# A fused two-layer feed-forward kernel: one product, half of the next narrow product and the gate chain taken at other places of the main stage

## The chip, the cores and the metric

The kernel runs on 1 core of a Trainium2 chip. The metric is the device time of one execution in microseconds: 909.95 us for the kernel before, the median of 3 runs that lie between 909.25 and 910.49 us. The profile comes from one more execution. PE is the matmul engine TensorE (PEld its weight loads), DVE is VectorE, ACT is ScalarE, POOL is GpSimd, SP is the engine that issues most DMAs.

## The reference, cut to what matters

Two blocks act on x of 4096 tokens by 1024 features, in float32. Each is a "cond" layer and a routed adapter layer behind it, with a residual:

```python
x = x + L0_ffn(L0_cond(x))     # cond 0: codebook-quantised weight + low-rank part; ffn 0: base W, bias, top-2 of 8 experts
x = x + L1_ffn(L1_cond(x))     # cond 1: weight, bias, an adapter per sequence of 64 tokens; ffn 1: base W, top-2 of 8 experts

# each routed layer
base   = x @ W.T (+ b)
logits = x @ W_router.T
rw, sel = top_k(logits, 2); rw = softmax(rw)
out    = base + sum over the two experts of rw * (x @ A[e].T) @ B[e] * 2
```

The first cond weight is quantised with `searchsorted` against thresholds made of the 64-entry codebook, in groups of 128 scaled by `exp(scale_log)`.

## The kernel before

Everything that does not depend on the gates is linear, so the kernel first multiplies the weights together: a 1024 x 1024 matrix G (`g_hi`, `g_lo`) and a narrow matrix `gx` with the router and adapter columns. This setup takes the first part of the span. In it, the codebook is brought from one row to all partitions by three groups of tiny matmuls (`codebook_step`, lines 546 to 555) that stand between the matmuls of an ordinary row product; `CB_AT` says behind which chunk. The product `delta(0)` behind that row waits for the copies that VectorE makes of them (`comp_ok`).

Float32 is kept by splitting each operand into a high and a low part (`fp32r`); a product a*b is three matmuls, hi*hi, hi*lo and lo*hi. ScalarE makes the high parts (line 978), VectorE the low ones (line 1310).

**The main stage** takes tiles of T2 = 256 tokens, numbered tau = 0 to 15. Tiles 0 and 1 are plain products. From tau = 2 on (`REG`), `winograd_products` computes a 2 x 2 block product with seven block products in place of eight. Each has 12 matmuls of 512 columns (line 858):

- i = 0 to 11, bank 3: the first of three products with a precomputed block T, which is read back from DRAM. There is room for one T, in two halves (`t_hi`, `t_lo`), so the halves are reloaded three times a tile. PE tells SP by `t_free`, six counts a tile, when a half can be overwritten; SP's program issues the loads (`load_t`) in order between the loads of x and the stores of the output.
- i = 12 to 23, bank 0; i = 24 to 35, bank 3.
- i = 36 to 47, bank 2: the second T product, with `m0_terms` (line 841) ahead and behind it.
- i = 48 to 59, bank 0 again: what this document calls the fifth product. It waits for ScalarE's copy of bank 0 (`p1_ok`).
- i = 60 to 71, bank 1.
- i = 72 to 83, bank 3: the third T product. Behind it VectorE makes a sum of bank 3 (line 1888, `u3_ok`), which waits for `t_free`.

**The gate chain** (`chain`, table `CHAIN`) is threaded into these products by the number i: a transposition of the gated values `m0` (line 775), six narrow matmuls that add them to the narrow banks (788 to 792), a transposition of the per-sequence low-rank values (799), and their product (807). Between these stand ScalarE's and VectorE's steps; the VectorE function `front` (lines 1725 to 1755) does the first gate's top-2 and softmax, `back` (to 1778) the second one's.

**The narrow product** `x_product(tau + 1)` (lines 519 to 521) has 48 matmuls of 304 columns and fills both narrow banks for the next tile. `front(tau + 1)` begins when it is done (`xx_mm`). It stands behind `low_terms` and the transposition of the second gate's values (`mid_turn`, line 775) and ahead of `mid_terms` (932 to 934), which end the tile.

The order on each engine is the order of the code, tile after tile. VectorE's main loop from line 1867 on reads: `m0_low`, `low_rank`, a sum of two partial products, the low part of half the next x, `u4_sum`, `back`, the low part of the other half, the sum behind the third T product (1888), `s_sums` (1821 to 1824, four sums of the next x), `mid_low`, `s_low` (1310), `front` of the next tile, and the output sums (1835) of which the first lies within `front`. ScalarE's loop has `x_high(tau + 1, 1)`, which waits for the fifth product (`p2_mm`), and then `rex`, the exponential in the middle of `back`.

Of the kernel before, what the change touches and what calls it, by code (L numbers as in the profile page):

```python
# [15 lines left out]
KC = D // P  # L16
# [18 lines left out]
CHAIN = [(30, 44, 62, 76), (10, 24, 42, 56), (12, 28, 44, 56)]  # L35
# [13 lines left out]
CB_AT = {(1, 0): 0, (1, 2): 1, (1, 6): 2}  # L49
# [13 lines left out]
def build(nc, xq, wall, m1t, aallt, x0t, b0t, lb1, lorabt, loraa, wq, cbook, ids, packed, out,  # L63
          e_dram, p1_dram, b_dram, t_dram):
    with ExitStack() as ctx:
# [217 lines left out]
        t_free, p1_mm, p2_mm, p6_mm = sem("t_free"), sem("p1_mm"), sem("p2_mm"), sem("p6_mm")  # L283
# [231 lines left out]
        def _(pe):  # L515
# [244 lines left out]
            def x_product(tau):  # L760

                u = tau if tau < REG else 0
                pe.wait_ge(x_hi_s, 2 * tau + 2)
                pe.wait_ge(x_lo_s, 2 * tau + 2)
                pe.wait_ge(gsel_ok, tau + 1)
                for b in range(2):
                    cs, ts = slice(SX * b, SX * b + WX), slice(b * P, b * P + P)
                    for c in range(KC):
                        mm = split_product(xb[:, b, cs], x_hi[u][:, c, ts], x_lo[u][:, c, ts],
                                           gx[:, c, cs], gx[:, 9 + c, cs], c == 0, c == KC - 1)  # L770
                mm.then_inc(xx_mm, 1)
# [71 lines left out]
            def winograd_products(tau):  # L843
# [43 lines left out]

                pe.wait_ge(ev[2], tau)
                m0_terms(2, True)
                t_loaded(0, 1)  # L890
                product(36, 2, quarter(0, 1, 1), (t_hi, t_lo), False, lambda: t_loaded(1, 1)).then_inc(t_free, 1)
# [3 lines left out]
                pe.wait_ge(p1_ok, n + 1)  # L895
                product(48, 0, quarter(0, 0, 1), g_quarter(1, 0), False).then_inc(p2_mm, 1)

                product(60, 1, quarter(1, 0, 1), g_quarter(1, 1), False)
# [50 lines left out]
            for tau in range(REG, NT2):  # L949
                winograd_products(tau)  # L950
                if tau + 1 < NT2:
                    low_terms(tau, (0, 2, 1))
                    mid_turn(tau)
                    low_terms(tau, (3,))
                    x_product(tau + 1)
                    mid_ready(tau)
                    mid_terms()
            last = NT2 - 1
            mid_turn(last)
# [15 lines left out]
        def _(act):  # L975
# [203 lines left out]
            def x_high(tau, k):  # L1179
# [3 lines left out]
                elif tau == REG:  # L1183
                    act.wait_ge(g_all, 1)
                else:
                    act.wait_ge(p2_mm if k else p1_mm, tau - REG)
# [76 lines left out]
            for tau in range(REG, NT2):  # L1263
# [15 lines left out]
                low_turned(tau)  # L1279
                if tau + 1 < NT2:  # L1280
                    x_high(tau + 1, 1)
                rex(tau, 1)
# [677 lines left out]
```

## Time and profile before

| | |
|---|---|
| median of 3 runs | 909.95 us |
| the profiled execution's own time | 910.41 us |
| span, first to last instruction | 908.7 us |
| PE busy | 902.7 us, 99% |
| PEld busy | 787.7 us, 87% |
| DVE busy | 616.3 us, 68% |
| ACT busy | 312.9 us, 34% |
| POOL busy | 145.7 us, 16% |
| granted TensorE clock | 1.0 of full speed in all slices |
| main stage from tau = 2 to 15 | from 433 us to 908 us |

A matmul's busy time overlaps that of the next one: the 512-column matmuls show a mean of about 395 ns and start some 230 ns apart. So the busy share says only that PE hardly ever waits; where time goes or comes from is read from the start times. A tile of the main stage takes about 34 us.

### The profile page before, as it was taken

What the parts mean: (1) busy time and instruction counts of PE and PEld (TensorE: products, weight loads), DVE (VectorE), ACT (ScalarE), POOL (GpSimd) and SP (SyncE); (2) the same over time, 40 slices, a digit from 0 to 9 for tenths busy, and PEclk for the clock granted to TensorE, in tenths of its full rate; (3) what the DMA queues carried; (4) which work ended last, traced back from release to release, by engine and by line L of the source; (5) the groups of instructions that cost most, each with busy time, mean ns of one, the idle gap of its engine ahead of it and who ended that gap; (6) DMA issues with size and microseconds to landing.
All of it is one profiled execution on the core that took longest, in us unless ns stands there. A gap on an engine that the chain in (4) does not pass through costs nothing.

```text
span 908.7 us, 13371 instructions
## 1 busy us (share of the span) xinstructions
PE 902.7 (99%) x4673; PEld 787.7 (87%) x4673; DVE 616.3 (68%) x1312; ACT 312.9 (34%) x503; POOL 145.7 (16%) x298
## 2 busy tenths in 40 slices
PE   9999999999999999999999999999999999999998
PEld 8999998888998888888888888888888888888886
DVE  6889899766587878976455565566566566566563
ACT  6578778411324334231321221222222222222220
POOL 0100010111011001414213213213113113113110
PEclk9999999999999999999999999999999999999999
DMA  9523330765412033657787787888888887877865
GB/s 360 188 82 114 120 125 23 257 193 186 142 50 93 8 131 102 212 208 238 268 290 260 270 285 255 279 277 258 285 276 262 283 272 261 286 268 265 287 221 188
DMA packets 60256, 191.45 MB, mean 211 GB/s; under 512 B 7681, under 2 KB 10394, under 8 KB 58270
## 3 DMA queue, kind: packets, MB, share of 16 engines
q1 hardware_dynamic: 49468, 158.99, 50.7%
q0 software_dynamic: 10432, 31.35, 11.3%
q8 instruction: 37, 0.61, 0.3%
q10 hardware_dynamic: 290, 0.26, 0.1%
q14 instruction: 29, 0.24, 0.1%
HBM read 158.86 MB, written 32.23 MB: 210 GB/s over the span
## 4 chain that ended last, share of the span: by engine, by line
PE 94%; DMA 4%; DVE 1%; SPq 1%; issue 0%; ACT 0%
PE bank L858 28%; PE bank L519 15%; PE bank L521 15%; PE bank L520 15%; PE bank L841 5%; PE bank L832 5%; DMA t_lo<-t_scratch 3%; PE bank L666 2%; PE bank L906 2%; PE bank L933 2%; PE bank L932 2%; PE bank L934 2%; DMA w_raw<-wall 1%; PE bank L775 1%; SPq L311 0%; PE bank L537 0%
## 5 line engine op out<-in xcount | busy, mean ns | idle before, releaser
L858 PE MATMUL bank<-g_hi,xs 128*128 128x512 f32 x448 | 145.2, 395 | 0.0
L858 PE MATMUL bank<-t_hi,xs 128*128 128x512 f32 x336 | 113.4, 396 | 0.6 <-DMA t_lo<-t_scratch 0.3
L490 POOL DMA_DIRECT2D p1sel<-p_scratch x128 | 65.6, 512 | 279.1 <-issue 279.0
L858 PEld LDWEIGHTS bank<-g_hi,xs 128*128 128x128 f32 x448 | 83.2, 188 | 16.4
L858 PE MATMUL bank<-g_lo,xs 128*128 128x512 f32 x224 | 88.2, 394 | 0.0
L978 ACT ACTIVATE xs<-x_raw 128x1024 fp32r<-128x1024 f32 x60 | 61.9, 1056 | 76.1 <-PE bank L858 55.8
L1310 DVE TENSOR_TENSOR xs<-x_raw,xs 128x1024 fp32r<-128x1024 f32 x60 | 75.1, 1273 | 12.0 <-ACT xs L978 11.5
L519 PE MATMUL bank<-gx,xs 128*128 128x304 f32 x256 | 77.4, 302 | 0.0
L521 PE MATMUL bank<-gx,xs 128*128 128x304 f32 x256 | 77.4, 302 | 0.0
L520 PE MATMUL bank<-gx,xs 128*128 128x304 f32 x256 | 77.3, 302 | 0.0
L858 PEld LDWEIGHTS bank<-t_hi,xs 128*128 128x128 f32 x336 | 62.0, 188 | 15.6 <-DMA t_lo<-t_scratch 3.2
L1725 DVE COPY rt<-bank 128x16 f32<-128x16 f32 x32 | 5.6, 174 | 99.0 <-PE bank L807 61.6
L501 POOL COPY bls<-bl 128x16 f32 x64 | 32.4, 506 | 249.0 <-ACT l L978 147.1
L519 PE MATMUL bank<-m_hi,w_hi 128*128 128x388 f32 (+1 forms) x192 | 65.9, 343 | 0.0
L858 PE MATMUL bank<-t_lo,xs 128*128 128x512 f32 x168 | 65.7, 391 | 0.0
L520 PE MATMUL bank<-m_lo,w_hi 128*128 128x388 f32 (+1 forms) x192 | 65.0, 339 | 0.0
L521 PE MATMUL bank<-m_hi,w_lo 128*128 128x388 f32 (+1 forms) x192 | 65.0, 338 | 0.0
L1471 DVE SCALAR_TENSOR_TENSOR rbuf<-qbuf,thr,rbuf 128x1024 f32<-128x1024 f32 x48 | 59.5, 1281 | 4.9 <-ACT rbuf L1029 4.3
L1029 ACT ACTIVATE rbuf<-rbuf,step 128x1024 f32<-128x1024 f32 x48 | 53.8, 1149 | 10.3 <-DVE rbuf L1466 6.8
L519 PE MATMUL bank<-weff_hi,w_hi 128*128 128x512 f32 x128 | 50.3, 393 | 0.0
L521 PE MATMUL bank<-weff_hi,w_lo 128*128 128x512 f32 x128 | 49.9, 390 | 0.0
L520 PE MATMUL bank<-weff_lo,w_hi 128*128 128x512 f32 x128 | 49.8, 389 | 0.0
(325 smaller groups left out, 2061.4 us busy)
## 6 DMA issues: line engine op xcount, KB each, us to landing
t_hi<-t_scratch SPq DMA_DIRECT2D x82, 512.0 KB, 4.5
t_lo<-t_scratch SPq DMA_DIRECT2D x82, 512.0 KB, 5.8
x_raw<-xq SPq DMA_DIRECT2D x16, 1024.0 KB, 6.7
out<-ost SPq DMA_DIRECT2D x63, 256.0 KB, 5.1
p1sel<-p_scratch POOLq DMA_DIRECT2D x64, 192.0 KB, 4.6
w_raw<-wall SPq DMA_DIRECT2D x16, 512.0 KB, 4.9
w<-e_scratch SPq DMA_DIRECT2D x6, 1024.0 KB, 5.1
ea<-e_scratch POOLq DMA_DIRECT2D x8, 644.0 KB, 4.5
```

The costliest lines, as they stand in the source:

```text
L490: pool.dma_start(f(p1sel[b][STK * s:STK * s + STK, cs]), p1_dram[bass.ds(i * STK, STK), cs]).then_inc(sems[b], 16)
L501: nc.gpsimd.tensor_copy(bls[:, b, s, :], bl[:, i, :].squeeze(1))
L519: nc.tensor.matmul(out_ap, lhs_hi, rhs_hi, start=first, stop=False, skip_group_check=True)
L520: nc.tensor.matmul(out_ap, lhs_hi, rhs_lo, start=False, stop=False, skip_group_check=True)
L521: return nc.tensor.matmul(out_ap, lhs_lo, rhs_hi, start=False, stop=last, skip_group_check=True)
L832: mm = nc.tensor.matmul(bk[j][:], l[tau][:, c, b * P:b * P + P], m[:, c, hs], start=c + k == 0, stop=c + k == KC + 1, skip_group_check=True)
L841: nc.tensor.matmul(bk[j][:], vt(l, b), m[:, hs], start=first and k == 0, stop=k == 2, skip_group_check=True)
L858: mm = nc.tensor.matmul(bk[j][:], l[:, c, :], m[:, c, :], start=first and c + k == 0, stop=c + k == KH + 1, skip_group_check=True)
L978: return nc.scalar.activation(dst, src, ACT.Identity)
L1029: nc.scalar.activation(rbuf[u][:], rbuf[u][:], ACT.Identity, bias=step[:, m:m + 1]).then_inc(a_ready[u], 1)
L1310: return nc.vector.tensor_tensor(dst, src, f(hi), ALU.subtract)
L1471: nc.vector.scalar_tensor_tensor(rbuf[u][:], qbuf[u][:], thr[:, m:m + 1], rbuf[u][:], ALU.is_gt, ALU.mult).then_inc(r_ready[u], 1)
```

## The change

- The fifth product (bank 0) is taken third of its row: at i = 36, ahead of the second T product, which goes from i = 36 to i = 48.
- `mid_turn(tau)` and the first half of `x_product(tau + 1)` (24 of its 48 matmuls, the first four chunks of both halves of the tile) come ahead of the last product, the third T product. The second half stays at the old place.
- The main stage's gate chain goes from (12, 28, 44, 56) to (12, 20, 34, 44).
- ScalarE: the high part of the second half of the next x now waits for `t_free` (end of the second T product) in place of `p2_mm`, and stands behind `rex(tau, 1)`.
- The codebook steps go from behind chunks 0, 2, 6 of their row to behind chunks 2, 4, 7.

```diff
-CHAIN = [(30, 44, 62, 76), (10, 24, 42, 56), (12, 28, 44, 56)]
+CHAIN = [(30, 44, 62, 76), (10, 24, 42, 56), (12, 20, 34, 44)]
-CB_AT = {(1, 0): 0, (1, 2): 1, (1, 6): 2}
+CB_AT = {(1, 2): 0, (1, 4): 1, (1, 7): 2}
...
-            def x_product(tau):
-
-                u = tau if tau < REG else 0
-                pe.wait_ge(x_hi_s, 2 * tau + 2)
-                pe.wait_ge(x_lo_s, 2 * tau + 2)
+            def x_product(tau, halves=(0, 1)):
+
+                u, last = tau if tau < REG else 0, KH * halves[-1] + KH
+                pe.wait_ge(x_hi_s, 2 * tau + halves[-1] + 1)
+                pe.wait_ge(x_lo_s, 2 * tau + halves[-1] + 1)
                 pe.wait_ge(gsel_ok, tau + 1)
                 for b in range(2):
                     cs, ts = slice(SX * b, SX * b + WX), slice(b * P, b * P + P)
-                    for c in range(KC):
+                    for c in range(KH * halves[0], last):
                         mm = split_product(xb[:, b, cs], x_hi[u][:, c, ts], x_lo[u][:, c, ts],
                                            gx[:, c, cs], gx[:, 9 + c, cs], c == 0, c == KC - 1)
-                mm.then_inc(xx_mm, 1)
+                if last == KC:
+                    mm.then_inc(xx_mm, 1)
...
+                pe.wait_ge(p1_ok, n + 1)
+                product(36, 0, quarter(0, 0, 1), g_quarter(1, 0), False)
+
                 pe.wait_ge(ev[2], tau)
                 m0_terms(2, True)
                 t_loaded(0, 1)
-                product(36, 2, quarter(0, 1, 1), (t_hi, t_lo), False, lambda: t_loaded(1, 1)).then_inc(t_free, 1)
+                product(48, 2, quarter(0, 1, 1), (t_hi, t_lo), False, lambda: t_loaded(1, 1)).then_inc(t_free, 1)
                 pe.wait_ge(ev[1], tau)
                 m0_terms(1, True)
 
-                pe.wait_ge(p1_ok, n + 1)
-                product(48, 0, quarter(0, 0, 1), g_quarter(1, 0), False).then_inc(p2_mm, 1)
-
                 product(60, 1, quarter(1, 0, 1), g_quarter(1, 1), False)
+
+                mid_turn(tau)
+                if tau + 1 < NT2:
+                    x_product(tau + 1, (0,))
 
                 pe.wait_ge(u4_ok, n + 1)
                 t_loaded(0, 2)
...
             for tau in range(REG, NT2):
                 winograd_products(tau)
                 if tau + 1 < NT2:
-                    low_terms(tau, (0, 2, 1))
-                    mid_turn(tau)
-                    low_terms(tau, (3,))
-                    x_product(tau + 1)
+                    low_terms(tau, (0, 2, 1, 3))
+                    x_product(tau + 1, (1,))
                     mid_ready(tau)
                     mid_terms()
             last = NT2 - 1
-            mid_turn(last)
...
+                elif k:
+                    act.wait_ge(t_free, 6 * (tau - REG) - 2)
                 else:
-                    act.wait_ge(p2_mm if k else p1_mm, tau - REG)
+                    act.wait_ge(p1_mm, tau - REG)
...
                 low_turned(tau)
+                rex(tau, 1)
                 if tau + 1 < NT2:
                     x_high(tau + 1, 1)
-                rex(tau, 1)
```

PE before, the end of a tile of the main stage: the last matmul of the third T product, the low-rank terms (906), the transposition of the second gate's values (775) and the start of the narrow product (519 to 521, 48 matmuls).

```order
L858 MATMUL bank<-t_hi,xs 128x512
L841 MATMUL bank<-p_hi,m0t_hi 128x512 [waits ld_p1w_1,ld_p1w_0]
L841 MATMUL bank<-p_lo,m0t_hi 128x512
L841 MATMUL bank<-p_hi,m0t_lo 128x512
L906 MATMUL bank<-p1sel_122,lowt 128x512
L775 MATMUL bank<-pk,midv 128x128 [waits mid_s]
L841 MATMUL bank<-p_hi,m0t_hi 128x512 [waits u3_ok]
L906 MATMUL bank<-p1sel_123,lowt 128x512
L519 MATMUL bank<-gx,xs 128x304 [waits gsel_ok,x_lo_s,x_hi_s]
```

PE now, at the same place, from the end of the product ahead of the third T product on (line 859 is what was 858, 776 was 775, 842 was 841, 911 was 906). Repeated rows within a product are left out.

```order
L859 MATMUL bank<-g_hi,xs 128x512
L776 MATMUL bank<-pk,midv 128x128 [waits mid_s]
L519 MATMUL bank<-gx,xs 128x304 [waits gsel_ok,x_lo_s,x_hi_s]
L521 MATMUL bank<-gx,xs 128x304
L859 MATMUL bank<-t_hi,xs 128x512 [waits ld_t0,u4_ok]
L859 MATMUL bank<-t_hi,xs 128x512 [waits ld_t1]
L842 MATMUL bank<-p_hi,m0t_hi 128x512 [waits ld_p1w_1,ld_p1w_0]
L911 MATMUL bank<-p1sel_122,lowt 128x512
L842 MATMUL bank<-p_hi,m0t_hi 128x512 [waits u3_ok]
L911 MATMUL bank<-p1sel_123,lowt 128x512
L519 MATMUL bank<-gx,xs 128x304 [waits gsel_ok,x_lo_s,x_hi_s]
```

The transposition and 24 narrow matmuls have moved from behind the third T product to ahead of it; 24 narrow matmuls are left between it and the end of the narrow product.

VectorE at that place, whose order is the same before and now: from the low part of the next x over the sum behind the third T product (1888) to the first operations of `front`.

```order
L1310 TENSOR_TENSOR xs<-x_raw,xs 128x4x256 [waits x_hi_s]
L1888 TENSOR_TENSOR p_sum<-bank,p_sum 128x512 [waits t_free]
L1821 TENSOR_TENSOR x_raw<-x_raw 128x4x128 [waits x_lo_s]
L1822 TENSOR_TENSOR x_raw<-x_raw 128x4x128 [waits dve_step]
L1824 TENSOR_TENSOR x_raw<-x_raw 128x4x128 [waits dve_step]
L1310 TENSOR_TENSOR midt_lo<-bank,midt_hi 128x256 [waits midt_hi_s]
L1310 TENSOR_TENSOR xs<-x_raw,xs 128x8x128 [waits s_hi_s] x2
L1725 COPY rt_157<-bank 128x16 [waits xx_mm]
```

Nothing has moved here; only what `t_free` and `xx_mm` stand behind on PE has.

ScalarE before, from its copy of bank 0 (1275) to the high part of the second gate's values:

```order
L1275 ACTIVATE p_sum<-bank 128x512 [waits p1_mm,ev3]
L978 ACTIVATE l_135<-lraw 64x2x16x2 [waits lraw_s]
L978 ACTIVATE xs<-x_raw 128x4x256 [waits p1_mm,ld_x]
L978 ACTIVATE lowt<-bank 98x256 [waits t1_mm]
L978 ACTIVATE xs<-x_raw 128x4x256 [waits p2_mm,ld_x]
L1200 ACTIVATE rs_2_163<-rs_2_163 128x2 [waits dif_ok]
L978 ACTIVATE midt_hi<-bank 128x256 [waits t2_mm]
```

ScalarE now (980 is what was 978, 1204 was 1200, 1279 was 1275):

```order
L1279 ACTIVATE p_sum<-bank 128x512 [waits p1_mm,ev3]
L980 ACTIVATE l_135<-lraw 64x2x16x2 [waits lraw_s]
L980 ACTIVATE xs<-x_raw 128x4x256 [waits p1_mm,ld_x]
L980 ACTIVATE lowt<-bank 98x256 [waits t1_mm]
L1204 ACTIVATE rs_2_163<-rs_2_163 128x2 [waits dif_ok]
L980 ACTIVATE xs<-x_raw 128x4x256 [waits t_free,ld_x]
L980 ACTIVATE midt_hi<-bank 128x256 [waits t2_mm]
```

The exponential has changed places with the high part of the second half of x, whose wait is another one.

## Rows read from the trace of the kernel before

**Rows 1.** Stretches, one a tile: us, busy PE, PEld, DVE, ACT, POOL, clock, DMA, GB/s.
```profile
467.55:501.91 34.36, 34.32 (x176) 29.11 (x175) 19.96 (x61) 7.79 (x14) 6.98 (x16) 1.00 0.82 276
...
535.94:570.55 34.61, 34.30 (x176) 29.11 (x175) 19.73 (x61) 7.78 (x14) 7.22 (x16) 1.00 0.79 270
...
843.93:878.00 34.07, 34.07 (x176) 29.21 (x174) 19.97 (x61) 7.78 (x14) 6.73 (x16) 1.00 0.76 249
sum 410.45, PE 409.85 PEld 349.87 DVE 239.47 ACT 93.39 POOL 86.16; mean PE 34.15 PEld 29.16 DVE 19.96 ACT 7.78 POOL 7.18
```
**Rows 2.** Waits: us in total, times, longest.
```profile
DVE rt L1725 <- PE bank L521: 37.5, 16, 3.0
PEld bank L858 <- DMA t_lo<-t_scratch: 3.2, 7, 0.7
```
**Rows 3.** Timeline, weight load of the second T product's second half; start, us.
```profile
821.07 0.19 PEld L858 LDWEIGHTS bank<-t_hi,xs 128*128 128x128 f32 x1 [0.55 <-DMA t_lo<-t_scratch]
```
**Rows 4.** Timeline of PE, from the third T product's last matmul on.
```profile
592.37 0.40 PE L858 MATMUL bank<-t_hi,xs 128*128 128x512 f32 x1
...
594.01 0.38 PE L775 MATMUL bank<-pk,midv 128*128 128x128 f32 x2
...
594.46 0.39 PE L841 MATMUL bank<-p_lo,m0t_hi 128*128 128x512 f32 x1
...
595.16 0.30 PE L519 MATMUL bank<-gx,xs 128*128 128x304 f32 x1
...
601.73 0.30 PE L521 MATMUL bank<-gx,xs 128*128 128x304 f32 x1
601.86 0.39 PE L932 MATMUL bank<-lb_hi,midt_hi 128*128 128x512 f32 x1
...
604.61 0.39 PE L858 MATMUL bank<-t_hi,xs 128*128 128x512 f32 x1
...
607.34 0.27 PE L775 MATMUL bank<-pk,m 128*128 128x128 f32 x1
```
**Rows 5.** Timeline of DVE beside it, in brackets its idle time.
```profile
590.72 1.22 DVE L1310 TENSOR_TENSOR xs<-x_raw,xs 128x1024 fp32r<-128x1024 f32 x1
592.81 0.69 DVE L1888 TENSOR_TENSOR p_sum<-bank,p_sum 128x512 f32<-128x512 f32 x1 [0.87 <-PE bank L858]
593.41 0.68 DVE L1821 TENSOR_TENSOR x_raw<-x_raw 128x512 f32<-128x512 f32 x1
...
597.40 2.36 DVE L1310 TENSOR_TENSOR xs<-x_raw,xs 128x1024 fp32r<-128x1024 f32 x2 [0.79 <-ACT xs L978]
602.06 0.17 DVE L1725 COPY rt<-bank 128x16 f32<-128x16 f32 x1 [2.30 <-PE bank L521]
...
606.70 0.42 DVE L1755 TENSOR_TENSOR m<-bank,rt 128x256 f32<-128x256 f32 x1
```
**Rows 6.** Timeline of PEld, the weight load of the first gate's transposition.
```profile
607.24 0.14 PEld L775 LDWEIGHTS bank<-pk,m 128*128 128x128 f32 x1 [0.16 <-issue]
```
**Rows 7.** Timeline of the gate chain's next steps.
```profile
610.57 0.60 ACT L1275 ACTIVATE p_sum<-bank 128x512 f32<-128x512 f32 x1 [1.94 <-PE bank L858]
612.45 0.53 ACT L978 ACTIVATE l<-lraw 64x64 fp32r<-64x64 f32 x2 [1.28 <-DVE lraw L1765]
613.01 0.42 DVE L1310 TENSOR_TENSOR l<-lraw,l 64x32 fp32r<-64x32 f32 x2 [0.59 <-ACT l L978]
```
**Rows 8.** Timeline of the codebook steps.
```profile
26.70 0.27 PE L546 MATMUL bank<-one,tt__169 1*64 1x1 f32 x2 [0.46 <-DVE cnt L1385]
30.90 0.88 PE L555 MATMUL bank<-selm,cols 64*128 64x64 f32 x6
32.45 0.47 PE L537 MATMUL bank<-la_hi,lb_hl 128*128 128x512 f32 x1
```
**Rows 9.** DMA issue by SP, and landing times of `t_lo` over the run.
```profile
593.16 0.43 SPq L411 DMA_DIRECT2D t_lo<-t_scratch  x1
DMA to landing us min/median/max: 3.6/5.9/9.1
```

## The prediction on record

> **What bounds the kernel now.** I read the stretches first, one for each tile of the main stage [rows 1]. In a tile that is not disturbed PE is busy for 34.07 us of 34.07, VectorE for 19.97, ScalarE for 7.78, at a granted clock of 1.00. So PE sets the time, and the main stage can only get shorter by what PE waits. The twelve stretches shown by their first and last sum to 410.45 us, 34.20 us a tile, more than the 34.07 of the undisturbed one; some are longer, up to 34.61. The list of waits says why [rows 2]: the weight loads waited seven times for the reload of T. The timeline puts such a wait in the middle of the second T product [rows 3]: the weights for its second half were not there, and the load sat idle for 0.55 us.
>
> Then the waits of the other engines, because the change moves what they are released by. VectorE waits 16 times for the end of the narrow product, 37.5 us in all [rows 2], so 2.3 us each time before it can begin `front`. That idle time costs nothing today. It is the quantity on which this forecast rests.
>
> How PE's work and VectorE's lie beside each other at a tile's end is in [rows 4, 5]. The third T product's last matmul starts at 592.37; VectorE's sum behind it starts at 592.81, then come four sums of x, a low part, and the low parts that end at 597.40 + 2.36 = 599.76. It is then idle for 2.30 us until the narrow product is done and `front` starts at 602.06. `front` ends at 606.70 + 0.42 = 607.12, and PE transposes its result at 607.34.
>
> **Part 1, the second T product goes from i = 36 to i = 48.** T is free for its reload at the same time as before, and is wanted 12 matmuls later; twelve such matmuls take 604.61 - 601.86 = 2.75 us, 0.23 each [rows 4]. The waits cost a tile at most 34.61 - 34.07 = 0.54 us. They all go. Gain: over the twelve stretches 410.45 - 12 x 34.07 = 1.6 us [rows 1]; with two tiles outside them at the same rate 1.8 us. The reload for the third T product showed no wait; between release and need it loses the 2.75 us of the fifth product and gains the 3.57 us of part 2. Nothing is late there.
>
> **Part 2, half of the narrow product and `mid_turn` ahead of the third T product.** PE has the same instructions, so the move costs PE nothing by itself. What it shifts is the end of the third T product. The narrow product's 48 matmuls take 601.86 - 595.16 = 6.70 us, half of them 3.35 us; the transposition takes 594.46 - 594.01 less one matmul of 0.23, so 0.22 us [rows 4]. The third T product therefore ends 3.35 + 0.22 = 3.57 us later in the tile, while the end of the narrow product stays where it is.
>
> VectorE's string from the sum to the start of `front` hangs on the end of the T product, and nothing in it was made shorter: 599.76 - 592.81 = 6.95 us, less 0.09 by which a successor starts before its forerunner's end, so 6.86 us [rows 5] (the sum of 0.69 at 592.81 has its successor at 593.41). It ends at 599.67 + 3.57 = 603.24 in the old tile's time, and `front` was due at 602.06. So `front` starts 603.24 - 602.06 = 1.18 us late: the 2.3 us of idle time are used up and 1.2 us are over.
>
> What waits for `front`? First the output sum within it, which frees bank 3 for the next tile's first product; then the transposition of `m0` at i = 12. Its place in `CHAIN` is unchanged. The transposition starts 607.34 - 607.12 = 0.22 us after `front` ends, and its weight load starts at 607.24 after 0.16 us of idle time, where the loads ahead of it follow without a gap [rows 4, 6]: the load already comes just when its input is there. I take the slack as 0.0 (it could be up to 0.1). So PE loses about 1.18 us a tile, some at the first matmul of the tile and the rest at i = 12, and all behind moves by that. The loss comes back each tile, since the next third T product moves along with PE. `front` of tiles 3 to 15 stands behind such a string: 13 times 1.18 = 15.3 us.
>
> Two things bound this from both sides. If the slack at the transposition were 0.1 us and some operation of the string 0.1 us quicker, it would be 13 x 1.0 = 13.0 us. If each restart of PE behind a wait costs another 0.1 us (a weight load of 0.19 us stands open, [rows 3] shows one of that length), it is 13 x 1.3 = 16.9 us. I keep 15.3, as the rows give it.
>
> Could VectorE take `front` ahead of the late string? After the low part of x ended at 590.72 + 1.22 = 591.94 it had all it needed for the first of the four sums, and yet that sum ran only at 593.41, behind the sum at 592.81 that waited 0.87 us for PE [rows 5]. So it keeps its program's order, and the late string holds `front` up. The Trainium skill (TensorE: Matmul & The Clock Gate, on the array's architecture) says the same of VectorE and ScalarE, strict first in, first out, and that PE alone may pull weight loads forward; by that rule, the trace agrees, the move costs its full 1.18 us, and without it it would cost nothing.
>
> **Part 3, the gate chain's steps moved up.** The six narrow matmuls now come at i = 20, before ScalarE's copy of bank 0 is due, so that copy starts up to 6 x 0.14 = 0.84 us later than the 3.23 us behind the transposition that it has now (610.57 - 607.34) [rows 4, 7]. Its 0.60, the high parts of 0.53 and the low parts of 0.42 us follow one another, so the low-rank values are ready about 5.5 us behind the transposition. PE comes to i = 34 after 22 matmuls of 0.23, the six and the transposition: 6.0 us. Slack some 0.3 us: cost 0. If that cover were gone by 0.3 us, 14 tiles would lose 4 us. The second gate, `back`, takes as long as `front` without the output sum, 5.06 - 0.69 = 4.4 us [rows 5], and its result is now wanted 28 product matmuls and 6 of `m0_terms` behind i = 44, 34 x 0.23 = 7.8 us: no wait. That `rex` stands ahead of the high part that now waits for the second T product keeps `back` from hanging on it: cost 0.
>
> **Part 4, loads.** VectorE's string also releases the load of the next x, which moves 3.57 us later; it starts at 603.3 in the old tile's time and is wanted behind the high parts of 0.53, some 5 us behind the transposition at 607.34 + 1.2, so 10 us later; the longest landing time of a T half is 9.1 [rows 9]. The first T of the next tile is reloaded 3.57 us later: its last quarter is issued at 593.16 + 3.57 = 596.73 and with the median of 5.9 us lands at 602.6, with the longest at 605.8, and is wanted at 604.61 + 6 x 0.23 = 606.0 or, with PE held up, later. Cost 0.
>
> **Part 5, codebook.** PE waited 0.46 us at the first step, which goes. But the product behind the row waits for VectorE's copies of the last step: 32.45 - 30.90 = 1.55 us after that step's start [rows 8]. The last step now has one chunk more ahead of it (3 matmuls of 0.18 = 0.53 us) and the 0.46 less, so it starts at about the same time, and the product with it. The gain is given back: 0, at most 0.1 either way.
>
> **Sum.** 15.3 - 1.8 = 13.5 us. On the profiled execution's own 910.41 us that gives 923.9; the median of the runs is 0.46 us below it, so 923.4 us.
>
> **The rivals.**
>
> *The VectorE string is covered, only the T wait goes* (the other side). VectorE is busy for only 58% of a tile [rows 1], so one might expect it to catch up. It would need the string of 6.86 us to shrink to 5.7, as it would if the 0.79 us that it waits within it for ScalarE's high part and 0.4 more went; but that high part is itself released by the four sums and shifts along. From 5.7 us on the cost is 0, and the time is 909.95 - 1.8 = 908.1 us. A string shorter by 0.8 gives 909.95 + 13 x 0.4 - 1.8 = 913.
>
> *The moved chain becomes a wait of its own.* The slack of 0.3 us at i = 34 is the smallest that I found beside `front`. If it is missed by 0.3 us, 14 x 0.3 = 4 us come on top: 927.4 us. For it speaks that ScalarE's string has no gap; against it, that every operation of it has the same length from tile to tile (twelve tiles have VectorE busy for 19.96 us in the mean, 19.97 in the last).
>
> *The first T's reload is late.* Today the second T has some 8.5 us from release to need (30 product matmuls of 0.23, with the chain's and `m0_terms` between them) and is up to 0.54 us late; the first T will have 606.0 - 592.6 - 3.57 = 9.8, plus PE's own delay, but beside it now run the small low-rank loads and x. If it is late by what the second was, 1.8 us in all, most lies beside the wait for `front`: 923.4 to 925.2 us. The Trainium skill (DMA: Bandwidth & Descriptors, on issuing engines) says that transfers from all queues share the same 16 engines and interleave; here the DMA share of a tile is 0.76 to 0.82, and nothing shown says how much a transfer loses by its neighbours.
>
> **How the numbers follow.** The forecast (slower, 13 x 1.0 to 1.3, T's waits gone, with or without a late first T): 0.80. The chain as a wait of its own: 0.10, 926 to 930 us. String partly covered, 911 to 919: 0.03. Covered: 0.06. No difference: 0.01. The likeliest gives 923.4 us. Its own range is 921 to 925.5; with the chain's case, and a little of the half-way case, 919 to 929.5. What can be told from no change is about 0.2%, 1.8 us: faster 0.06, same 0.01, slower 0.93.
>
> **What would show it.** Right: VectorE's copy at the head of `front` no longer waits for the narrow product (37.5 us fall to under 10, those left being the plain tiles); a stretch of a tile is 35.2 us; PE shows a wait for VectorE at the first T product's start and at the transposition of `m0`, together 1.2 us; no wait for T in the second T product; the codebook's 0.46 us gone and the start of the product behind it unchanged. Wrong: VectorE still idle before `front`, or a tile of 34.05 us, or one over 35.6 us with a wait at i = 34 or for T.

## The result, and the profile after

The changed kernel takes 925.08 us (median of 6 runs, 924.17 to 926.68), the kernel before 910.12 us beside it (6 runs, 909.25 to 910.62): a ratio of 1.0168, 95% interval 1.0157 to 1.0179. It is slower by 1.7%. The forecast was 923.4 us. The profiled execution of after took 925.21 us with a span of 923.5, against 908.7 before: 14.8 us to account for. The granted clock is 1.00 in the mean of both.

One tile of the main stage after, in the columns of [rows 1]:

```profile
573.51:608.69 35.18, 34.56 (x174) 29.07 (x174) 19.72 (x61) 7.66 (x14) 7.27 (x16) 1.00 0.78 261
```

Starts of successive tiles lie 35.17 us apart in the mean of twelve, where they were 34.20 apart (34.05 where nothing disturbed). Thirteen tiles at 0.97 us more are 12.6 us; 2.2 us are still to be found, and they are not in these tiles.

The list of waits of after (us in total, times, longest one):

```profile
DVE rt L1729 <- PE bank L521: 7.3, 3, 3.0
PEld bank L859 <- DVE ost L1839: 11.1, 13, 0.9
PE bank L859 <- DVE ost L1839: 5.6, 13, 0.4
PE bank L776 <- DVE m L1759: 2.2, 12, 0.2
```

VectorE's wait for the end of the narrow product has fallen from 37.5 us in 16 times to 7.3 in 3 [rows 2], and PE has new waits in their place, one pair a tile: at the next tile's first product and at the transposition of `m0` (L776). VectorE's timeline around one end of a tile (start, us, in brackets the idle time before):

```profile
599.84 0.69 DVE L1892 TENSOR_TENSOR p_sum<-bank,p_sum 128x512 f32<-128x512 f32 x1 [7.38 <-PE bank L859]
...
604.43 2.36 DVE L1314 TENSOR_TENSOR xs<-x_raw,xs 128x1024 fp32r<-128x1024 f32 x2 [0.79 <-ACT xs L980]
606.71 0.17 DVE L1729 COPY rt<-bank 128x16 f32<-128x16 f32 x1
607.95 0.69 DVE L1839 TENSOR_TENSOR ost<-bank,p_sum 128x512 f32<-128x512 f32 x1
...
611.33 0.42 DVE L1759 TENSOR_TENSOR m<-bank,rt 128x256 f32<-128x256 f32 x1
```

and PE's beside it:

```profile
599.41 0.39 PE L859 MATMUL bank<-t_hi,xs 128*128 128x512 f32 x1
...
605.19 0.30 PE L521 MATMUL bank<-gx,xs 128*128 128x304 f32 x1
...
608.69 0.50 PE L859 MATMUL bank<-t_hi,xs 128*128 128x512 f32 x1 [0.43 <-DVE ost L1839]
...
611.90 0.41 PE L776 MATMUL bank<-pk,m 128*128 128x128 f32 x2 [0.19 <-DVE m L1759]
```

Read them against [rows 4, 5]. The third T product ends with the matmul at 599.41, and VectorE's sum behind it starts at 599.84: the string of 6.87 us up to the copy at 606.71 is as long as it was (6.86). The last narrow matmul starts at 605.19. Before, the copy came 0.33 us behind such a matmul (602.06 - 601.73, the row of it being in [rows 4]); now it would be due at 605.52 and starts at 606.71, 1.19 us late and with no idle time ahead of it. Two things wait for it: the next tile's first product, 0.43 us at its matmul, for the output sum at 607.95; and the transposition of `m0` at 611.90, for `front`'s last operation, which ends at 611.33 + 0.42 = 611.75. That last gap is 0.15 us where it was 0.22, so there was slack of 0.07 us, and PE loses 1.12 us a tile (35.17 - 34.05), not the whole 1.19.

The other 2.2 us stand in the last tile, in the middle of its third T product (PE and its weight loads):

```profile
913.66 0.19 PEld L859 LDWEIGHTS bank<-t_hi,xs 128*128 128x128 f32 x1 [2.46 <-DMA t_lo<-t_scratch]
913.66 0.50 PE L859 MATMUL bank<-t_hi,xs 128*128 128x512 f32 x1 [2.03 <-DMA t_lo<-t_scratch]
```

and the transfer that it waited for was issued at

```profile
906.97 0.43 SPq L411 DMA_DIRECT2D t_lo<-t_scratch  x1
```

so 6.7 us ahead of that weight load, while the median of such a transfer in after is 6.5 us from issue to landing (the row stands further down). It was not slow, it was needed too early. In every other tile half of the narrow product, 3.35 us, stands between the release of T and the third T product; in the last tile there is no next x and so no narrow product.

The codebook, finally. Before, PE waited 0.46 us at the first step and the product behind the row began at 32.45 [rows 8]. After:

```profile
27.12 0.27 PE L546 MATMUL bank<-one,tt__169 1*64 1x1 f32 x2
...
30.80 0.88 PE L555 MATMUL bank<-selm,cols 64*128 64x64 f32 x6
...
32.35 0.47 PE L537 MATMUL bank<-la_hi,lb_hl 128*128 128x512 f32 x1 [0.67 <-DVE valid L1403]
```

The wait at the first step is gone and the last step comes at the same time, and the product behind it waits for VectorE instead: 0.10 us earlier.

The sum of this reading: 13 x 1.12 = 14.6 for the late `front`, 2.0 back from T's waits (12.6 = 14.6 - 2.0), 2.2 in the last tile: 14.8 us. The 2.2 is what the tiles leave over; 2.03 of it is seen as PE's idle time, and an experiment below takes it away.

### The profile page after: what moved, and what is told of

It is laid out like the page before. It is cut to its first block, busy times and chain, and to the rows that moved or that the text cites. A ratio compares the mean times of both kernels' runs of the same rounds, so it can differ in the third digit from the quotient of the medians.

```text
span 923.5 us, 13384 instructions
## 1 busy us (share of the span) xinstructions
PE 907.2 (98%) x4673; PEld 786.1 (85%) x4673; DVE 614.8 (67%) x1312; ACT 311.4 (34%) x503; POOL 144.6 (16%) x298
## 4 chain that ended last, share of the span: by engine, by line
PE 80%; DVE 14%; ACT 2%; DMA 2%; issue 1%; SPq 0%
PE bank L859 25%; PE bank L519 13%; PE bank L520 13%; PE bank L521 13%; PE bank L833 5%; DVE xs L1314 3%; PE bank L842 3%; PE bank L666 2%; ACT xs L980 2%; PE bank L776 1%; DVE x_raw L1828 1%; DVE x_raw L1827 1%; DVE x_raw L1826 1%; DVE ost L1839 1%; DVE p_sum L1892 1%
## 5 line engine op out<-in xcount | busy, mean ns | idle before, releaser
L859 PE MATMUL bank<-g_hi,xs 128*128 128x512 f32 x448 | 145.9, 397 | 0.0
L859 PE MATMUL bank<-t_hi,xs 128*128 128x512 f32 x336 | 112.8, 396 | 7.7 <-DVE ost L1839 5.6
L859 PEld LDWEIGHTS bank<-g_hi,xs 128*128 128x128 f32 x448 | 82.2, 188 | 15.1
L1314 DVE TENSOR_TENSOR xs<-x_raw,xs 128x1024 fp32r<-128x1024 f32 x60 | 72.8, 1235 | 25.5 <-ACT xs L980 25.0
L859 PE MATMUL bank<-g_lo,xs 128*128 128x512 f32 x224 | 88.8, 397 | 0.0
L859 PEld LDWEIGHTS bank<-t_hi,xs 128*128 128x128 f32 x336 | 63.1, 188 | 26.5 <-DVE ost L1839 11.1
L1892 DVE TENSOR_TENSOR p_sum<-bank,p_sum 128x512 f32<-128x512 f32 x14 | 9.7, 691 | 104.6 <-PE bank L859 104.6
L859 PE MATMUL bank<-t_lo,xs 128*128 128x512 f32 x168 | 65.7, 391 | 0.0
L501 POOL COPY bls<-bl 128x16 f32 x64 | 29.6, 462 | 219.6 <-issue 204.5
L1204 ACT ACTIVATE rs<-rs 128x2 f32<-128x2 f32 x32 | 6.5, 203 | 142.8 <-DVE rs L1743 142.8
```

What stands on the lines that cost most here:

```text
L501: nc.gpsimd.tensor_copy(bls[:, b, s, :], bl[:, i, :].squeeze(1))
L859: mm = nc.tensor.matmul(bk[j][:], l[:, c, :], m[:, c, :], start=first and c + k == 0, stop=c + k == KH + 1, skip_group_check=True)
L1314: return nc.vector.tensor_tensor(dst, src, f(hi), ALU.subtract)
```

## The experiments

Theory: VectorE's string behind the third T product is 1.2 us too long for what is left of the narrow product, and that is the tile's whole loss; the last tile is a matter of its own; chain and codebook cost nothing. Rivals: PE loses at the tile's end for another reason (the loads, or the first gate's chain), and the string only happens to end there; and the last tile's wait is covered by something else and returns elsewhere if it is taken away.

**One repair for each cause.** The first leaves every product where the change put it and moves VectorE's own work: the sums of x (`s_sums`) and the low part of the middle value (`mid_low`), which need nothing of the third T product, go ahead of the operation that waits for it.

```
+                if tau + 1 < NT2:
+                    s_sums(tau + 1)
+                mid_low(tau)
                 v.wait_ge(t_free, 6 * n + 6)
                 nc.vector.tensor_tensor(p5_sum[:], bk[3][:], p5_sum[:], ALU.add).then_inc(u3_ok, 1)
-                if tau + 1 < NT2:
-                    s_sums(tau + 1)
-                mid_low(tau)
```

> The changed kernel with two steps of VectorE's order moved: s_sums and mid_low come ahead of the sum behind the third T product, into the 7.4 us that VectorE now idles there. Theory A: the string behind the T product is then the sum (0.6), ScalarE's high parts (2.0, beside it) and two low parts that end some 3.5 us behind it, under the 5.7 us until the narrow product is done; front is on time, all 13 waits at the tile's head go: 925.1 - 14.6 = 910.5 us (909.5 to 911.5), the last tile's wait of 2.2 us left. Rival (PE's wait at the tile's head comes from the output store, the x load or the moved chain rather than from this string): 925 us, or a new wait in its place, 915 to 925.

Measured: 910.71 us (11 runs), ratio 1.0014 (1.0005 to 1.0023). Its waits and VectorE's timeline at one end of a tile:

```profile
DVE rt L1729 <- PE bank L521: 35.2, 16, 3.0
PEld bank L859 <- DMA t_lo<-t_scratch: 1.7, 1, 1.7
```

```profile
588.10 0.69 DVE L1825 TENSOR_TENSOR x_raw<-x_raw 128x512 f32<-128x512 f32 x1
...
595.44 0.69 DVE L1895 TENSOR_TENSOR p_sum<-bank,p_sum 128x512 f32<-128x512 f32 x1 [4.13 <-PE bank L859]
596.60 2.36 DVE L1314 TENSOR_TENSOR xs<-x_raw,xs 128x1024 fp32r<-128x1024 f32 x2 [0.46 <-ACT xs L980]
601.13 0.18 DVE L1729 COPY rt<-bank 128x16 f32<-128x16 f32 x1 [2.18 <-PE bank L521]
```

The first sum of x now runs in the time in which VectorE stood idle for the T product, the string behind the sum at 595.44 is down to two operations, and the copy again waits 2.18 us for PE. All thirteen waits of PE for VectorE are gone, and so are 925.08 - 910.71 = 14.4 us. The edit moves one load as well: that of the next x is released at the end of this string and now starts 3.5 us behind the sum (598.98 against 595.44), where it started 7.0 us behind it (606.82 against 599.84). The median time to landing of these loads grew from 7.6 to 9.6 us, and yet PE waits for no load in these tiles; so late loads were not the reason. The one wait for T that remains is the last tile's, 1.25 us at the matmul in this run.

The second repair is for the last tile alone: there the products go in the old order (the edit, shortened).

```
+                if tau + 1 < NT2:
                     product(36, 0, ...); m0_terms(2, True); product(48, 2, ... T ...); m0_terms(1, True)
+                else:
+                    m0_terms(2, True); product(36, 2, ... T ...); m0_terms(1, True); product(48, 0, ...)
```

> The changed kernel with the old product order in the last tile alone, which has no narrow product to cover the third T's reload. Theory A: the wait of 2.0 to 2.4 us before the second half of the last T product goes; at most 0.2 us come back at the second T: 925.1 - 2.2 = 922.9 us. Rival (in the last tile the end is set by something behind the T product, its outputs' stores): 925.1 us.

Measured: 922.89 us (4 runs), ratio 1.0144 (1.0129 to 1.0160), 2.2 us less than after, and no wait for T left in its list.

Both together, the version to which the experiments point:

> Both repairs in one kernel: VectorE's s_sums and mid_low ahead of the sum behind the third T product, and the old product order in the last tile. Theory A (the two losses are separate, 14.4 and 2.2 us, and the gain on the second T's waits stays): 925.1 - 14.4 - 2.2 = 908.5 us, 1.6 us under the kernel before, all tiles about 34.05 us. Rival (the second T's waits come back, since with front on time the loads begin closer together): 910 us, same as before.

Measured: 908.77 us (11 runs, 908.61 to 909.39) against 910.32, ratio 0.9986 (0.9977 to 0.9995). It beats both kernels, the one before by 0.14%, a small gain but outside the interval. VectorE's timeline, the same operation of `front` in two tiles that follow each other:

```profile
470.04 0.42 DVE L1770 TENSOR_TENSOR m<-bank,rt 128x256 f32<-128x256 f32 x1
504.12 0.42 DVE L1770 TENSOR_TENSOR m<-bank,rt 128x256 f32<-128x256 f32 x1
```

That is 34.08 us, and the other tiles of this kernel take the same within 0.03, where those of before took from 34.03 to 34.61: what T's waits cost before, 1.8 to 2 us, has come back, less some 0.03 us a tile.

**The string's arithmetic, by its length.** A quarter and three quarters of the narrow product ahead of the third T product, in place of a half (`x_product(tau + 1, (0, k))`, k = 2 and 6 of its 8 chunks). By the string alone, a quarter shifts the T product by 1.90 us and must be free, three quarters by 5.25 us and must cost 1.68 us a tile more than the half.

> The changed kernel with 12 in place of 24 of the 48 narrow matmuls ahead of the third T product (two chunks of eight). The third T product ends 1.68 + 0.22 = 1.9 us later than in the kernel before, less than VectorE's 2.3 us of idle time. Theory A: VectorE's string is on time and PE does not wait for it; but T's third reload is covered by 1.7 us less, so a wait for T of some 1.0 us a tile takes its place (2.9 us a tile with nothing moved, less 1.9): 910.1 + 13 + 2.2 - 1.8 = 923.5 us (920 to 926), with waits for T and none for VectorE. Rival (any part of the narrow product ahead of the T product costs the same 1.1 us, by a restart or by its banks): waits for VectorE as in the changed kernel, 925 us or more.

Measured: 917.72 us (4 runs), ratio 1.0083 (1.0067 to 1.0098).

```profile
DVE rt L1729 <- PE bank L521: 11.7, 16, 3.0
PE bank L859 <- DMA t_lo<-t_scratch: 5.4, 11, 1.2
```

VectorE is in time, with some 0.4 us to spare a tile, as worked out; the waits for T stand where expected, in the third T product, but are smaller than I had put them (5.4 us at the matmuls, against some 15): the time was missed by 6 us.

> The changed kernel with 36 in place of 24 narrow matmuls ahead of the third T product. Theory A: VectorE's string ends another 1.68 us later against the end of the narrow product, and all of it is loss, 13 x 1.68 = 21.8 us: 925.1 + 21.8 = 946.9 us (945 to 949), front 2.9 us late, no wait for T but the last tile's. Rival (the loss is fixed per tile, or comes from a transfer): 925 us.

Measured: 956.38 us (4 runs), ratio 1.0546 (1.0498 to 1.0594). The waits are the expected ones (`PEld bank L859 <- DVE ost L1839` at 30.6 us in 13 times), and 9.5 us more are lost than expected. The stretches behind one of them (us, busy PE, PEld, DVE, ACT, POOL, granted clock, DMA, GB/s) and PE at its end:

```profile
506.49:508.00 1.51, 1.51 (x4) 1.24 (x5) 1.05 (x7) 0.22 (x2) 0.00 (x0) 0.59 0.91 312
508.00:510.00 2.00, 2.00 (x6) 1.54 (x6) 1.81 (x8) 0.47 (x1) 0.00 (x0) 0.50 0.98 302
510.00:512.00 2.00, 2.00 (x11) 1.64 (x10) 0.98 (x3) 0.66 (x2) 0.00 (x0) 0.95 1.04 372
```

```profile
506.49 0.58 PE L859 MATMUL bank<-t_hi,xs 128*128 128x512 f32 x1 [1.93 <-DVE ost L1839]
506.86 0.63 PE L859 MATMUL bank<-t_lo,xs 128*128 128x512 f32 x1
507.29 1.06 PE L859 MATMUL bank<-t_hi,xs 128*128 128x512 f32 x2
```

PE stood idle for 1.93 us, and 0.3 us behind its restart the clock is granted at 0.50, its 1.2 GHz level: matmuls come 0.43 us apart where they come 0.23 apart at 2.4 GHz. It stays so for 3.4 us. This happened behind 7 of the 13 such waits, all of them of 1.9 us, and the mean clock of the run is 0.987: 954 x 0.013 = 12 us. Against after, PE's waits at the first product grew by 25.1 - 5.6 = 19.5 us and those at the transposition of `m0` shrank by 1.5; with the clock that makes 30.4 of the 30.5 us between the two profiled spans.

**The second gate's chain**, set back to (12, 28, 44, 56) in after.

> The changed kernel with the gate chain at its old steps (12, 28, 44, 56). The second gate's product then stands at i = 56, in the second T product; from there to mid_turn it is only 4 + 12 matmuls and 3 of m0_terms, 4.4 us, and back takes 4.4 us on VectorE behind 0.4 us of latencies and 0.2 us ahead of the transposition. So mid_turn waits some 0.6 us in 14 tiles, on top of the wait for front: 925.1 + 8 = 933 us (929 to 937). Rival (the chain's steps are free either way, slack everywhere): 925 us. Rival (the moved chain is part of the loss): under 925 us.

Measured: 929.63 us (4 runs), ratio 1.0218 (1.0203 to 1.0234). The new wait:

```profile
PEld bank L776 <- DVE midv L1782: 7.9, 14, 0.6
```

It is where and as large as expected, at the weight load of the second transposition that now stands early in the tile; but a weight load runs ahead of its matmul (in this run the load at 594.55 is that of the matmul at 594.77), and the matmuls lost only some 0.32 us each, 4.5 us in all and not 8. So the moved chain is not a refinement but a part of the change: without it the early `mid_turn` waits. And since in after neither transposition nor narrow matmul of this chain waits, the prediction's "cost 0" holds.

**Half the narrow product alone**: after with the old order of the products and the old codebook places.

> The changed kernel with the products in the old order (second T product at i = 36) and the codebook steps at their old places: the half narrow product and mid_turn stay early, with the new chain. Theory A: front is 1.2 us late in 13 tiles as before (+14.6), the last tile's wait for the third T goes (third T again 2.75 us later), and the second T's waits come back (1.8 us, or more since its loads begin behind a later output store): 910.1 + 14.6 + 0 to 3 = 925 to 928 us. Rival B (the product's move costs): the loss goes, 910 us. A late transfer as the cause of the loss at a tile's head would show as a wait for a DMA there; theory A has a wait for VectorE.

Measured: 930.19 us (4 runs), ratio 1.0238 (1.0214 to 1.0262). The wait for VectorE is the same to the tenth as in after (11.1 us, 13 times), so it belongs to this part. The waits for T, which the new order of the products would take away, are there, all in the second T product, and larger than in the kernel before (3.2 us in seven [rows 2]):

```profile
PEld bank L859 <- DMA t_lo<-t_scratch: 9.2, 12, 1.2
```

**The fifth product third, alone.** The narrow product, `mid_turn`, chain and codebook are those of before.

> The kernel before with one part of the change alone: the fifth product third, the second T product behind it. Narrow product, mid_turn, gate chain and codebook stand where they were. Theory A (VectorE's string behind the late third T product costs 1.12 us a tile, and the half narrow product ahead of that product also covers T's third reload): the string is on time again, VectorE waits 2.3 us for the narrow product, nothing is lost there; but the third T product now comes 2.75 us sooner behind the second, as in the last tile of the changed kernel, where it waited 2.0 to 2.4 us. So each of 14 tiles waits some 2.2 us for T: 910.1 + 31 - 1.8 = 939 us (935 to 943). Rival B (the product's move is what costs the 1.1 us a tile, the half narrow product is harmless, and the last tile's wait is special to it): 925 us, waits spread as in the changed kernel. Rival C (the product's move is pure gain): 908 us.

Measured: 963.79 us (4 runs), ratio 1.0591 (1.0565 to 1.0616), almost twice the expected loss. The list of waits, three of the waits in the middle of a third T product, and a stretch behind the second of the three:

```profile
PEld bank L859 <- DMA t_lo<-t_scratch: 40.0, 14, 3.3
```

```profile
531.84 0.50 PE L859 MATMUL bank<-t_hi,xs 128*128 128x512 f32 x1 [1.85 <-DMA t_lo<-t_scratch]
...
570.76 0.80 PE L859 MATMUL bank<-t_hi,xs 128*128 128x512 f32 x1 [2.83 <-DMA t_lo<-t_scratch]
...
649.71 0.50 PE L859 MATMUL bank<-t_hi,xs 128*128 128x512 f32 x1 [2.85 <-DMA t_lo<-t_scratch]
```

```profile
571.00:572.00 1.00, 1.00 (x3) 0.81 (x4) 0.00 (x0) 0.00 (x0) 0.00 (x0) 0.50 0.87 348
```

The place is the expected one: all 14 tiles now have what after has in its last tile alone, a reload of T that the fifth product no longer covers. The size is not. The idle time of each wait is 1.8 to 2.9 us, 2.4 in the mean, and at 8 of the 14 the clock was granted at 0.50 for a while, 3.4 us in six cases and 6.8 us in two (the one at 570.76 is of these). The mean clock is 0.982; up to 963 x 0.018 = 17 us were lost to it, beside the 34.7 us that PE's matmuls waited. The wait's length does not tell which: at 531.84 the clock fell behind 1.85 us, at 649.71 it stayed at 1.00 behind 2.85 us.

**The half narrow product with the repair, in the old order of the products.** Is the exchange of the products still needed once VectorE's string is mended?

> Half of the narrow product early and the new gate chain, the old product order, and VectorE's s_sums and mid_low ahead of the sum behind the third T product. VectorE's loss is gone, so what is over 908.8 us (both repairs, new product order) is what the second T's late reload costs: with waits as in the kernel before 910.3 us; with the larger ones of the half-narrow-product kernel with the old order (9.2 us of weight-load waits in 12 tiles) up to 913.5 us. Theory A: 910 to 913.5, all its waits for T. Rival (that kernel's extra 5 us came from VectorE, not from T): 908.8.

Measured: 919.52 us (8 runs), ratio 1.0093 (1.0062 to 1.0124), 6 us above the range expected. VectorE is in time again, and the loss is all for T. Its waits, and then its DMA issues between 467 and 880 us (how many, KB each, median us from issue to landing):

```profile
PEld bank L859 <- DMA t_lo<-t_scratch: 15.5, 18, 1.4
```

```profile
x_raw<-xq SPq DMA_DIRECT2D x11, 1024.0 KB, 9.6
t_lo<-t_scratch SPq DMA_DIRECT2D x70, 512.0 KB, 6.3
```

of before in the same stretch,

```profile
x_raw<-xq SPq DMA_DIRECT2D x11, 1024.0 KB, 6.5
t_lo<-t_scratch SPq DMA_DIRECT2D x72, 512.0 KB, 5.7
```

and of after:

```profile
x_raw<-xq SPq DMA_DIRECT2D x11, 1024.0 KB, 7.6
t_lo<-t_scratch SPq DMA_DIRECT2D x70, 512.0 KB, 6.5
```

and of the kernel with both repairs, which is this one with the products exchanged in all tiles but the last (and the codebook steps at their new places):

```profile
x_raw<-xq SPq DMA_DIRECT2D x11, 1024.0 KB, 9.5
t_lo<-t_scratch SPq DMA_DIRECT2D x73, 512.0 KB, 6.3
```

The loads land later than before in all three changed kernels, and no sooner with the products exchanged; yet in the tiles ahead of the last only this one waits for T, every time in the second T product. So what the exchange gives is not a faster reload but 2.75 us more until it is wanted. Beside the two repairs it is worth some 10.7 us (919.5 - 908.8, the kernels before beside them 0.4 us apart), beside the half narrow product alone 930.2 - 922.9 = 7.3 us (against the kernel with the last tile in the old order). Why the loads land later, and which neighbouring transfer costs how much, was not separated. The Trainium skill (DMA: Bandwidth & Descriptors, on issuing engines) has transfers of all queues share the same engines. These landing times are in keeping with that, but no run here isolates it.

**Three small ones.** After with only the low part of the middle value ahead of the waiting sum:

> The changed kernel with mid_low alone ahead of the sum behind the third T product (s_sums stay behind it). Theory A with one detail more: mid_low (0.42 us) lies within the 0.79 + 0.42 us that VectorE's string must wait for ScalarE's high part anyway, and that high part is released by the sums, so the string does not get shorter: 925.1 us (924.5 to 925.6). Rival (the string is the plain sum of its operations): 0.34 us a tile less, 13 x 0.34 = 4.4, 920.7 us. That s_sums, not mid_low, is what the repaired kernel gained by follows from the first.

Measured: 924.80 us (4 runs), ratio 1.0148 (1.0097 to 1.0200), no gain: the 0.42 us are moved, and the wait inside the string for ScalarE grows from 0.79 us to

```profile
604.35 2.36 DVE L1314 TENSOR_TENSOR xs<-x_raw,xs 128x1024 fp32r<-128x1024 f32 x2 [1.13 <-ACT xs L980]
```

What must get ahead are the sums of x, which ScalarE's high part hangs on. In the profiled run of this kernel PE's wait in the last tile was 1.83 us, and the clock fell behind it:

```profile
913.73 0.50 PE L859 MATMUL bank<-t_hi,xs 128*128 128x512 f32 x1 [1.83 <-DMA t_lo<-t_scratch]
914.58:916.00 1.42, 1.42 (x5) 1.13 (x4) 0.00 (x0) 0.00 (x0) 0.00 (x0) 0.50 0.00 0
```

That run took 926.90 us where the other three took 924.3 to 925.0. In after the same place, with 2.03 us of wait, kept the clock at 1.00.

The kernel before with its codebook steps moved back, nothing else:

> The kernel before with the codebook steps alone moved to chunks 2, 4, 7. Forecast: the first step's wait of 0.46 us goes and a wait for VectorE's copies of 0.6 to 0.7 us stands in front of the product behind the row: 910.1 us, no difference. Rival (the gain stays): 909.6, at the edge of what can be told; the start of that product (32.45 before) tells it apart: 31.9 if the gain stays, 32.4 if not.

Measured: 910.17 us (10 runs) against 909.96, ratio 0.9993 (0.9970 to 1.0016). The product behind the row begins at

```profile
32.33 0.47 PE L537 MATMUL bank<-la_hi,lb_hl 128*128 128x512 f32 x1 [0.67 <-DVE valid L1399]
```

where it began at 32.45, so the gain of 0.46 us is indeed given back. And the four sums alone put ahead on the kernel before:

> The kernel before with s_sums alone ahead of VectorE's sum behind the third T product. Theory A: it is no repair by itself. There the T product ends 0.9 us behind the low part of x, so the four sums (2.86 us, 591.85 to 594.71 in the tile of the rows) push the sum behind the T product from 592.81 to 594.62; its result is there at 595.3 where PE's m0_terms for bank 3 want it at 594.14, so PE waits 1.3 us in 13 tiles: 910 + 17 = 927 us (922 to 931), with waits for VectorE's p_sum. Rival (VectorE's order alone is what the repaired kernel gained by, whatever stands on PE): 908.5 to 910 us.

Measured: 927.28 us (4 runs), ratio 1.0193 (1.0174 to 1.0212).

```profile
PE bank L841 <- DVE p_sum L1890: 14.7, 13, 1.2
```

There the third T product ends 3.57 us earlier, the sums of x are still running when it does, and PE's `m0_terms` wait for the sum behind it. Moving the sums costs 18 us in the one kernel and saves 14 in the other.

## Why the prediction was right, and where it was not

**What bounds the kernel** held: PE, and the idle time of VectorE ahead of `front` was the quantity to count.

**VectorE's string** (13 x 1.18 = 15.3 us) was right as a mechanism and by 0.7 us too large. Experiment by experiment: the copy's wait for PE is gone, the waits sit at the first T product and at the transposition of `m0`, three quarters of the narrow product make them longer and a quarter makes them vanish, and the sums taken ahead, with the low part, remove 14.4 us with no other operation moved. The term that was mis-sized is the slack at the transposition, taken as 0.0 and allowed up to 0.1; it was 0.07, and the loss 1.12 us a tile.

**T's waits** (-1.8) was right for the sum of after, about -2.0. But it was a statement on this combination, not on the part: the prediction costed the exchange by the waits of before, while beside the half narrow product it is worth 7.3 us, for the waits for T that it takes away there are larger than those of before (9.2 us at the weight loads against 3.2). Alone it costs 54, the half narrow product alone 20, and together they cost 15. Parts that feed one set of transfers don't add.

**The loads** is the step that failed. "The reload for the third T product showed no wait; between release and need it loses the 2.75 us of the fifth product and gains the 3.57 us of part 2. Nothing is late there." True of 13 tiles. In the last there is no narrow product, so it loses 2.75 and gains only the 0.22 of `mid_turn`: 2.03 us of wait, 2.2 us in the time, removed by the one experiment that changes that tile alone. The edit itself shows it: `if tau + 1 < NT2` stands ahead of the part that covers. The string's size missed by 0.7 and T's by 0.2 to one side and this by 2.2 to the other make the 1.3 us between 923.9 and 925.2 for the profiled execution. That the number came so near is in part luck, since the errors partly cancel; that it came out slower by some 15 us is not, since the term that makes it was read off the rows and is borne out by itself.

The first T's reload, a rival, did not come late: after's list has no such wait in the tiles, and neither has that of the kernel with both repairs, where no wait for `front` could hide it.

**The chain** at 0 was right, with the cover at i = 34 as thin as forecast: in the tile shown the low-rank values are ready at 617.38 and their transposition starts at 617.94 without a wait (VectorE's L1314, PE's L800), so there is 0.56 us less the 0.15 to 0.22 us from VectorE to PE seen above. What setting the chain back costs, 4.5 us, is another place, the second gate's. **The codebook** at 0 was right: 0.1 us came of it, and alone on before it can't be told from nothing.

**In order**: that VectorE keeps to its program's order was the ground for counting the whole delay, and the repair shows it directly. The same operations in another order, released no earlier, saved 14.4 us.

## What to carry to other kernels

When a product that releases a string of work moves later, compare its shift with the idle time at the string's end, not with the engine's busy share, and then look in the string for what doesn't need the release: put ahead of it, that work brought a loss of 1.7% down to 0.14%, and with the last tile mended as well the kernel gained 0.14%. Such an order fits one placement only: the sums put ahead lost 18 us on the kernel before. Check each cover again in the iterations that lack it, the last above all: a move justified by "it loses this and gains that" holds only where "that" exists. Sum the parts of a change for the combination that runs; of parts that share transfers, each alone may be far worse than all together.

## What was not expected of the hardware

- **The clock can double a wait's price, and the wait's length does not say when.** Among waits of 1.8 to 2.9 us in dense work PE's granted clock fell to 0.50, its 1.2 GHz level, at 8 of 14 (products alone), at 7 of 13 of 1.9 us each (three quarters) and at the one of 1.83 us (`mid_low` alone), with matmuls 0.43 us apart instead of 0.23; it stayed at 1.00 behind after's 2.03 us and behind one of 2.85 us. Waits of 0.2 to 0.4 us (after) and of 1.1 to 1.2 us (13 times, the sums ahead on the kernel before) left it at 1.00. What decides between the cases is open; no run separated it.
- **A weight load's wait is not the matmul's.** 0.58 us of idle time at a load cost PE's matmuls 0.32 to 0.35, 0.86 cost 0.6 to 0.7.
- **From VectorE to PE** the gap between the end of the operation waited for and the start of the matmul, where PE really waited, was the same in all 13 tiles of after but not for both operations: 0.15 us behind `front`'s last one (`m`), 0.05 us behind the output sum (608.69 - 608.64). In before, where PE did not wait for `m`, it was 0.22.
- **The same transfers land later when other work is released at other times**: the median of the same 512 KB went from 5.7 to 6.5 us, that of 1 MB from 6.5 to 7.6 and 9.6, at a DMA share of 0.76 to 0.82 in before's tiles and 0.76 to 0.78 in after's. The cause was not separated.
